# Linear attention in a decoder layer: the causal mask from DVE to ACT and GpSimd, and half of each feature map from DVE to GpSimd

## The reference, cut to what matters

```python
def _feature_map(t, K):
    f = jnp.einsum('hdf,bhld->bhlf', K, t)
    feats = jnp.concatenate([jax.nn.softmax(f, axis=-1), jax.nn.softmax(-f, axis=-1)], axis=-1)
    return jnp.maximum(feats, EPS)
q = _heads(x @ Wq); k = _heads(x @ Wk); v = _heads(x @ Wv)
qf = _feature_map(q, Kq)
kf = _feature_map(k, Kk)
kv = jnp.cumsum(kf[:, :, :, None, :] * v[..., None], axis=2)
o = jnp.einsum('bhlf,bhldf->bhld', qf, kv)
z = jnp.einsum('bhlf,bhlf->bhl', qf, jnp.cumsum(kf, axis=2)) + EPS
o = o / z[..., None]
```

## Time and profile before

| | |
|---|---|
| median of 3 runs | 1231.16 us (1226.87 to 1235.7) |
| time of the profiled execution | 1229.25 us |
| its span in the trace | 1227.0 us |
| linear attention, first part of the span | to about 540 us |
| busy over the span: PE, DVE, ACT, POOL | 91%, 78%, 50%, 31% |
| mean granted clock of PE | 0.982 of full speed |

### The profile page before, as it was taken

The page is one execution under the profiler, slowest core; times in us unless marked ns, Lnnn a source line. Parts: engine busy times, 40 slices in busy tenths (PEclk is TensorE's granted clock), DMA queues, the critical chain, the costliest instruction groups (busy, mean ns, idle before and its releaser), DMA issues. The chain is left out here.

```text
span 1227.0 us, 30062 instructions
## 1 busy us (share of the span) xinstructions
PE 1117.3 (91%) x11860; PEld 719.6 (59%) x11861; DVE 962.1 (78%) x1769; ACT 611.1 (50%) x1166; POOL 377.3 (31%) x355
## 2 busy tenths in 40 slices
PE   6698898899899999879999999999999957999996
PEld 5577777777788878643443344334444334666765
DVE  6889978987888788888788677877889556777757
ACT  4233343334333433227777677776788822444443
POOL 4432245222522222113201320222110414656651
PEclk9899999999999999999999999999999988999998
DMA  7100001000400000524720570065050144221225
GB/s 240 41 8 1 2 28 53 2 1 1 80 2 2 1 1 2 81 59 81 152 34 8 114 146 2 9 127 108 2 211 3 53 80 145 65 64 60 63 62 205
DMA packets 60045, 73.65 MB, mean 60 GB/s; under 512 B 14404, under 2 KB 51140, under 8 KB 59188
## 3 DMA queue, kind: packets, MB, share of 16 engines
q1 hardware_dynamic: 56132, 61.56, 21.0%
q0 software_dynamic: 3792, 10.36, 2.7%
HBM read 52.86 MB, written 18.78 MB: 58 GB/s over the span
## 5 line engine op out<-in xcount | busy, mean ns | idle before, releaser
L1791 DVE TENSOR_REDUCE neg_max<-pS 128x1 f32<-128x1024 f32 x238 | 284.9, 1220 | 56.2 <-PE pS L1574 56.0
L1706 ACT ACTIVATE pt<-pR 128x512 f32<-128x512 f32 x512 | 286.5, 600 | 80.1 <-PE pR L1597 75.3
L1597 PE MATMUL pR<-qs,ks 100*32 100x512 bf16 x2048 | 191.2, 383 | 3.1 <-ACT pt L1706 1.6
L1574 PE MATMUL pS<-ks,qs 100*32 100x512 bf16 x1904 | 145.9, 381 | 5.1 <-issue 1.9
L1611 PE MATMUL b_pO<-pt,b_v 128*32 128x512 f32 x1024 | 135.9, 605 | 2.9 <-ACT pt L1706 2.3
L1597 PEld LDWEIGHTS pR<-qs,ks 100*32 100x32 bf16 x2048 | 56.2, 96 | 95.3 <-issue 25.6
L324 POOL TENSOR_TENSOR kf<-kf,fsum 128x2048 f32<-128x2048 f32 (+1 forms) x17 | 58.2, 3422 | 163.8 <-DVE fsum L933 163.8
L324 POOL TENSOR_TENSOR qs<-qs,fsum 128x2048 f32<-128x2048 f32 (+1 forms) x17 | 58.5, 3446 | 142.7 <-DVE fsum L933 142.7
L1453 POOL COPY qs<-max_rows 3x512 bf16<-3x512 bf16 x60 | 36.6, 610 | 209.3 <-ACT max_rows L1699 206.3
L745 ACT COPY qfT<-pT 128x512 f32<-128x512 f32 x64 | 37.3, 582 | 122.7 <-PE pT L466 122.7
L1574 PEld LDWEIGHTS pS<-ks,qs 100*32 100x32 bf16 x1904 | 51.4, 97 | 74.3 <-issue 35.7
(11 more groups left out here) (376 smaller groups left out, 2270.8 us busy)
## 6 DMA issues: line engine op xcount, KB each, us to landing
qs<-q_scr SPq DMA_DIRECT2D x24, 256.0 KB
ks<-k_scr SPq DMA_DIRECT2D x7, 768.0 KB
k_scr<-f SPq DMA_DIRECT2D x18, 256.0 KB, 2.8
ks<-in_L_ffn_w_dram SPq DMA_DIRECT2D x2, 2048.0 KB, 11.1
ks<-in_L_ffn_w_dram SPq DMA_DIRECT2D x4, 1024.0 KB, 8.5
ks<-y_rows SPq DMA_DIRECT2D x16, 256.0 KB, 5.1
ks<-k_scr SPq DMA_DIRECT2D x6, 512.0 KB
cx<-in_ctx_dram SPq DMA_DIRECT2D x3, 768.0 KB, 12.3
```

Source lines behind the costliest of these rows:

```text
L1574: ins = pe.matmul(pS1[q:q + XV, slot, 512 * half:512 * half + 512], qs[0:KR, bass.ds(par, 1), h, P * t + q:P * t + q + XV].rearrange("r a ...
L1597: ins = pe.matmul(ring[bank][q:q + XV, :], ks[0:KR, bass.ds(par, 1), h, P * j + q:P * j + q + XV].rearrange("r a n -> r (a n)"), qs[0:KR, ...
L1706: nc.scalar.activation(pt[:, j % 2, i, :], ring[bank], ACT.Exp).then_inc(exp_done, 1)
L1791: nc.vector.tensor_reduce(neg_max[:, hg % 2, u // G, u % G:u % G + 1], pS1[:, u % 2, :], AX_X, ALU.max, negate=True).then_inc(max_done, 1)
```

## The change

The mask is split in two. ACT copies the scores from PSUM into am (`scores_copy`, signal `a_copied`), and POOL multiplies am in place with the causal triangle (`mask`, signal `a_masked`). PE may write the next scores into pA after `a_copied`; `outputs` still waits for `a_masked`. Of the feature maps (from turn 2 on for k, from turn 1 on for q) DVE writes only f - max, together with the small difference min - max of each head (`low_less_high`); POOL's `other_side` subtracts the one from the other, which gives min - f, and signals `shifted`, on which the exponential waits. The bank is free for PE after DVE's part alone (`drained`). POOL's constants move from ahead of the first turn into it. ACT's `v_copy` of half 0 moves ahead of `scores_copy(t, 3)`.

```diff
+                def other_side(m, t, half_of, par):
+                    pool.wait_ge(drained[m], 2 * (t - POOL_FROM[m]) + half_of + 1)
+                    hs = slice(8 * half_of, 8 * half_of + 8)
+                    nc.gpsimd.tensor_tensor(feat[m][:, par, hs, HD:F2],
+                                            low_less_high[:, m, hs].unsqueeze(2).broadcast_to([P, H // 2, HD]),
+                                            feat[m][:, par, hs, 0:HD], ALU.subtract).then_inc(shifted[m], 1)
...
+                def mask(t, g):
+                    wait(pool, a_copied, 4 * t + g + 1)
+                    pool.wait_ge(s_k, 8)
+                    nc.gpsimd.tensor_tensor(am[:, g % 2], am[:, g % 2], causal[:, :].unsqueeze(1).broadcast_to([P, G, P]),
+                                            ALU.mult).then_inc(a_masked, 1)
+
+                mask(0, 0)
                 scale(0, 1, 1)
...
-                        if not (last and c == TB - 1):
-                            scale(1, TB * b + c + 1, (c + 1) % 2)
+                        t, par = TB * b + c, c % 2
+                        has1, has2 = not (last and c == TB - 1), not (last and c >= TB - 2)
+                        mask(t, 1)
+                        if has1:
+                            other_side(1, t + 1, 0, 1 - par)
+                            other_side(1, t + 1, 1, 1 - par)
+                        if (b, c) == (0, 0):
+                            constants()
+                        mask(t, 2)
+                        if has1:
+                            scale(1, t + 1, 1 - par)
+                        mask(t, 3)
                         if (b, c) == (0, TB - 1):
                             split_k(0)
                             split_k(1)
-                        if not (last and c >= TB - 2):
-                            scale(0, TB * b + c + 2, c % 2)
+                        if has2:
+                            other_side(0, t + 2, 0, par)
+                            other_side(0, t + 2, 1, par)
+                        if has1:
+                            mask(t + 1, 0)
+                        if has2:
+                            scale(0, t + 2, par)
                         if (b, c) == (0, TB - 1):
                             split_k(2)
                             split_k(3)
...
                 def project_q(t, half, par):
-                    wait(pe, shifted[0], 2 * t + half + 1)
+                    bank_drained(pe, 0, t, half)
...
                 def chunk_scores(t, g):
...
-                    wait(pe, a_masked, 4 * t + g)
+                    wait(pe, a_copied, 4 * t + g)
...
+                def scores_copy(t, g):
+                    wait(act, a_done, 4 * t + g + 1)
+                    wait(act, o_done, 4 * t + g - 1)
+                    nc.scalar.copy(am[:, g % 2], pA[:, :, :]).then_inc(a_copied, 1)
...
                         f_copies(t, 1)
+                        scores_copy(t, 1)
...
                         f_copies(t, 2)
                         if has1:
                             exponentials(1, t + 1, 0, 1 - par)
+                        scores_copy(t, 2)
...
-                    nc.vector.tensor_tensor(feat[m][:, par, hs, 0:HD], f,
-                                            hi[:, m, hs].unsqueeze(2).broadcast_to([P, H // 2, HD]), ALU.subtract)
+                    if t >= POOL_FROM[m]:
+                        nc.vector.tensor_tensor(low_less_high[:, m, hs], lo[:, m, hs], hi[:, m, hs], ALU.subtract)
+                    ins = nc.vector.tensor_tensor(feat[m][:, par, hs, 0:HD], f,
+                                                  hi[:, m, hs].unsqueeze(2).broadcast_to([P, H // 2, HD]),
+                                                  ALU.subtract)
+                    if t >= POOL_FROM[m]:
+                        ins.then_inc(drained[m], 1)
+                        return
...
-                            if g < G - 1:
-                                mask(t, g + 1)
...
-                        if has1:
-                            mask(t + 1, 0)
```

More of the change, by code:

```diff
@@ L100, in linear_attention @@
         lo = sb("lo", [P, 2, H])
+        low_less_high = sb("low_less_high", [P, 2, H])
         fsum = sb("fsum", [P, 2, 2 * H])
@@ L163, in linear_attention @@
         shifted = [sem("k_shifted"), sem("q_shifted")]
+        drained = [sem("k_drained"), sem("q_drained")]
         expd = [sem("k_exp"), sem("q_exp")]
@@ L169, in linear_attention @@
         fT_ready = [sem("kT"), sem("qT")]
-        a_done, a_masked = sem("a_done"), sem("a_masked")
+        a_done, a_copied, a_masked = sem("a_done"), sem("a_copied"), sem("a_masked")
         d_done, s_upd = sem("d_done"), sem("state")
@@ L214, in linear_attention, with bank_drained @@
         HALVES = (slice(0, H // 2), slice(H // 2, H))
+        POOL_FROM = (2, 1)
+        def bank_drained(eng, m, t, half_of):
+            if t < POOL_FROM[m]:
+                eng.wait_ge(shifted[m], 2 * t + half_of + 1)
+            else:
+                eng.wait_ge(drained[m], 2 * (t - POOL_FROM[m]) + half_of + 1)
         with nc.Block() as block:
@@ L330, in _ @@
                         scale(m, 0, 0, hs, half_of)
-                scale(0, 1, 1)
[L333 to L347, removed]
+                def mask(t, g):
[3 more added lines that the diff above has]
+                                            ALU.mult).then_inc(a_masked, 1)
@@ new lines, in _, with constants @@
+                mask(0, 0)
+                scale(0, 1, 1)
+                def constants():
+                    pool.memset(last_row[:, :], 0.0).then_inc(s_k, 1)
+                    pool.wait_ge(s_k, 9)
+                    pool.affine_select(out=last_row[:, :], in_=last_row[:, :], compare_op=ALU.not_equal, fill=1.0,
+                                       base=-(KR - 1), pattern=[[0, 1]], channel_multiplier=1).then_inc(s_k, 1)
+                    pool.memset(q_aug[:, :], 0.0).then_inc(s_k, 1)
+                    pool.memset(zero[:, :], 0.0).then_inc(s_k, 1)
+                    pool.memset(max_parts[:, :, :, :], 0.0).then_inc(s_k, 1)
+                    pool.wait_ge(s_k, 12)
+                    pool.wait_ge(s_c, 48)
+                    for s in range(2):
+                        nc.gpsimd.tensor_copy(ck[:, s, :].rearrange("p (d h) -> p d h", h=XH),
+                                              ck_raw[:, s, :].rearrange("p (h d) -> p d h", h=XH)).then_inc(c_turned, 1)
+                    for k in range(KD):
+                        nc.gpsimd.tensor_copy(cq[:, k, :].rearrange("p (d h) -> p d h", h=XH),
+                                              cq_raw[:, k, :].rearrange("p (h d) -> p d h", h=XH)).then_inc(c_turned, 1)
@@ L448, in project_q @@
                 def project_q(t, half, par):
-                    wait(pe, shifted[0], 2 * t + half + 1)
+                    bank_drained(pe, 0, t, half)
                     project(1, half, par, proj[1])
                 def project_v(t, half, par):
-                    wait(pe, shifted[1], 2 * t + half + 1)
+                    bank_drained(pe, 1, t, half)
                     project(2, half, par, v_proj)
@@ L589, in turn_maxima @@
                     pe.wait_ge(prep_copied, PREPARED + 1)
-                    pe.wait_ge(a_masked, 4 * T)
+                    pe.wait_ge(a_copied, 4 * T)
                     turned = pA[:, :, :].rearrange("p h n -> p (h n)")
@@ L799, in _ @@
                 f_copies(0, 0)
+                scores_copy(0, 0)
                 exponentials(0, 1, 1, 1)
@@ L817, in batch @@
                             exponentials(1, t + 1, 1, 1 - par)
+                            v_copy(t + 1, 0, 1 - par)
+                        scores_copy(t, 3)
                         prepare(prep, 4)
-                        if has1:
-                            v_copy(t + 1, 0, 1 - par)
                         prepare(prep, 5)
@@ L846, in batch @@
                             exponentials(0, t + 2, 1, par)
+                        if has1:
+                            scores_copy(t + 1, 0)
                 batch(0, False)
@@ L938, in clamp @@
                                             ALU.max).then_inc(f_ready[m], 1)
[L940 to L945, removed]
                 def update(b, c, g):
@@ L1070, in _ @@
                 shift(0, 1, 1, 1, own)
-                dve.wait_ge(s_k, 6)
-                mask(0, 0)
                 denominators(0, 1, 1, own)
```

## The result

The changed kernel takes 1310.4 us (median of four runs, 1309.62 to 1310.8) against 1231.01 us (1226.87 to 1235.7): ratio 1.0643, 95% interval 1.0604 to 1.0682. Forecast were 1291 us and a range of 1257 to 1316. The profiled execution took 1310.69 us with a span of 1308.5.

What follows compares the result with a forecast made beforehand. The prediction took PE to lead, losing time to DVE, and the change to delay each turn's last outputs through POOL's order. Terms of +51, -9, +14.5, +5, +2 and -2 gave +61.5 on 1229.25: 1291 us, range 1257 to 1316.

Steps and rivals of the forecast that it cites:

- O3: The last outputs of a turn (group 3) on PE, forecast 21.6 us into the turn against 18.2 before, +3.4.
- Behind O3: PE's part of a turn after O3: 11.1 us, claimed to stay because PE waits there only for x_rest (0.92).
- a rival at 0.13: PE's granted clock falls behind the new waits, 3.4 us each in 7 turns: +24, 1315 us; chance 0.13.
- the sum: Terms added over the attention turns: +51, -9, +14.5, +5, +2, -2, together +61.5 on 1229.25, making 1291 us.
- turns 4 and 8, splits: POOL's two splits ahead of the group 1 mask delay PE: +14.5 us for both turns, bounds 10 and 18.
- turns 5, 9, 13, power: The variance's power heads POOL's order, waits for DVE's x1_normalise and delays the group 1 mask: +1.7 each, +5 us.
- turn 0, beyond O3's delay: POOL's constants now stand ahead of turn 0's group 2 mask: +2 us.
- The chain to O3: Steps from k scaling through shift, other_side, exponential, sum, q scaling and group 3 mask, putting O3 at 21.6 us.
- The meetings at the port: DVE and POOL block each other: the small difference behind k scaling, other_side behind the clamp; without both, O3 about 19.4, +1.2.
- The rival that had no meetings: The small difference slips past POOL and other_side past the clamp: +30, 1259 us; chance 0.20.
- The relief of DVE: Rival: a shorter DVE removes PE's waits if q scaling starts by 12.0 us into the turn: 1209 us; chance 0.05.
- the two waits: PE's waits on DVE for the mask ahead of the next scores (8.8) and the state (7.5), some 16 us.

Runs made afterwards that it cites:

- PE kept busy: The changed kernel with extra transposes of the identity, which nobody reads, ahead of the outputs where PE waits for a mask: 1292.69 us.
- when spread: The changed kernel with the 24 steps of POOL's six splits set one to three at a time between the maps' instructions: 1296.09 us.
- the run with POOL's whole order: The changed kernel with only POOL's order changed: group 3 mask before q scaling, splits spread, power, constants and turn 0's group 1 mask moved: 1223.1 us.
- the sides alone: The changed kernel with masks back on DVE straight from PSUM, without ACT's copies; POOL still makes the maps' negative side: 1245.97 us.
- the masks alone: The changed kernel with both sides of the feature maps back on DVE; ACT still copies scores and POOL masks them: 1293.7 us.
- with the mask of group 3 first: The changed kernel with one line of POOL's order moved: the group 3 mask ahead of the next q map's scaling: 1250.84 us.
- the two fastest runs: POOL's whole order changed plus the minimum over the positive side replacing the difference: 1215.86 us; the same with DVE's x1_normalise step moved to turn 6: 1216.35 us.
- the better order: POOL's whole order changed, with the minimum and x1_normalise moved: 1216.35 us; beside it the same with masks back on DVE, without ACT's copies: 1237.05 us.

## Why the prediction came out as it did

The direction and the mechanism were right: POOL's order, not its load or DVE's, sets O3. Where the forecast fell short by 19 us is the step "Behind O3 PE waits only for `x_rest` (0.92), so these 11.1 us stay." They did not stay, because of the clock, which I had as a rival at 0.13 and left out of the sum. With PE kept busy the changed kernel takes 1292.7 us, where the sum without the clock said 1291; with that rival's +24 it said 1315, and 1310.4 came. That 1292.7 lies so near to 1291 is in part luck: the clock was still at 0.97 there, and O3's delay, which the sum had too long, and turn 0, which it had too short, offset each other. The price of 3.4 us a wait and seven turns was near to what the fills showed: 2.7 us in turn 10, and 2 to 3.3 us in seven turns. There is luck in this too, since the stretch of the earlier trace rows that gave the price holds a second wait, of 2.60 us at 51.15. I should have made it part of the forecast: the sum itself put a wait of 3.7 us into each turn, and the earlier trace rows showed what one wait of 5.2 did.

| step | forecast, us | shown, us |
|---|---|---|
| O3 after the turn's first transposes | 21.6 | 21.1 (21.1 with PE kept busy) |
| behind O3 | 11.1 | 13.8 (11.1 with PE kept busy) |
| turns 4 and 8, splits | +14.5 | 14.3 come back when spread, clock included |
| turns 5, 9, 13, power | +5 | about +3.5 |
| turn 0, beyond O3's delay | +2 | +4.6 (7.4 in all) |
| turn 11 | 0 | 0 (32.74 and 32.77) |
| turn 15 | -2 | -1.9 |
| clock | 0 | 17.7 or more |

*The chain to O3.* Its first steps came to 0.1 us: the scaling of k at 2.13 to 5.75 (forecast 2.2 to 5.8), the difference waiting until 5.8 (5.9). Then `shift` of half 1 started at 8.1 instead of 8.5, and the second `other_side` ended at 12.2 instead of 12.9; the mask took 1.26 where I had 1.16. So O3 comes +2.8 a turn instead of +3.4. With PE kept busy turns 6, 10 and 12 took 2.8 us longer than before from residual to residual, just this delay. Turns 1, 2, 3, 7, 11 and 14 took 0.0 to 2.6 longer, so that some 8 us were covered there; the sum had 9 covered. The rows of the table do not add up to the 79.4 us, since the clock stands in several of them.

*The meetings at the port.* They are there, as rows above show, and removing the first one gave 6.9 us. My bound without both, +1.2 a turn, took the first at 1.1 us and left out that `normalise` still meets POOL, which the sum itself had in it; O3 of turn 10 gained 0.7. The rival that had no meetings is refuted by the rows. Only the first of them was removed; what the clamp's meeting costs was not tried.

*Turn 0.* Its residual started at 91.58 instead of 84.23. I counted the constants by the mask of group 2 alone. In the trace that wait is 4.6 us long, and 3.6 of the 7.4 us came back in the run with POOL's whole order (residual at 87.98):

```profile
73.86 0.93 PE L543 MATMUL pO<-v,am 128*64 128x66 f32 x12 [4.64 <-POOL am L352]
```

The masks on POOL make most of it: with the sides alone the residual stood at 86.97, at a clock of 1.00 from 62 us on, and with the masks alone at 93.25, at 0.84 (the changed kernel: 0.88). How it divides between their waits and the clock was not tried.

*Turns 4 and 8.* PE stood 9.57 and 9.03 us at `outputs` of group 1 where I said 8. The sum counts 9.8 us for two splits, though 10.3 less 0.9 is 9.4. Turn 4's wait:

```profile
217.84 1.15 PE L543 MATMUL pO<-v,am 128*64 128x66 f32 x16 [9.57 <-POOL am L352]
```

*The power.* Turns 9 and 13 took 37.5 us from residual to residual where turns 10 and 12 took 34.8. Before, they were 0.5 and 1.0 us longer than these already, so that the power makes 2.2 and 1.6 of it; turn 5, 2.2 longer than turn 6 before and 1.9 after, shows none. Ahead of the masks, but with the mask of group 3 first, turns 9 and 13 took 31.6 and 31.5, with the power behind the mask of group 2 both took 28.6; turns 10 and 12 took some 28 in both runs.

*The relief of DVE.* The rival gave 1209 if O3 had its mask by 16.8 us into the turn, and put against it "every row of the chain". For the changed kernel that held. With the order mended (and the minimum in place of the difference) O3 of turn 10 stands at 16.78 and the time is 1216:

```profile
355.89:372.67 16.78, 16.78 (x237) 14.91 (x237) 14.60 (x26) 8.74 (x15) 13.09 (x8) 1.00 0.01 2
372.67:383.71 11.04, 10.11 (x91) 8.91 (x87) 7.25 (x13) 4.32 (x7) 4.30 (x3) 1.00 0.00 0
```

PE is busy through the whole first part. So the price of 20 us was near: the two fastest runs lie 16 and 21 us below the kernel before beside them, the run with the order alone 14. Its condition had a second way in, which I did not name: not an earlier scaling, but the mask ahead of it. The 16 us that I counted for the two waits left one line of PE's waits before out, the state's first update in a batch:

```profile
PE pDW L484 <- DVE state L952: 4.9, 6, 1.1
```

With it they are 21 us, and the masks on POOL gave 20.7 in the better order.

*The rest.* Of the signs that I had named, a turn of 32 to 33 us without special work failed: it took 34.8, and 32.1 with PE kept busy. PE's longest wait a turn (3.94, for POOL), the start of the q scaling (16.1 us into turn 10) and the mean of the difference held (0.65 us, here from 100 to 530 us):

```profile
L972 DVE TENSOR_TENSOR low_less_high<-lo,hi 128x8 f32<-128x8 f32 x47 | 30.3, 646 | 1.6
```

DVE's busy time over the span fell by 27.5 us (962.1 to 934.6) and not by 60. What it stands blocked makes most of that: these 47 instructions alone took 30.3 us, where 0.17 each would be 8. From the last residual to the end the kernel took 684 us after 688 before, and 684 to 690 in the experiments, so cross attention and experts kept their length.

## What to carry to other kernels

Where work moves to another engine, its place in that engine's order can count for more than its length: here the place of one line was worth 60 us, on an engine that was half idle. Put the short step for which PE waits ahead of the long one that has slack, and cut long blocks into steps. And where a forecast puts a wait into PE's path, it must also price the slow clock behind it: with waits of 3 to 4 us a turn here, that was a fifth of the whole loss or more.

## What the runs showed of the hardware

- Filling PE's waits with useless transposes made the kernel 17.7 us faster. Waits of 3.2 and 3.9 us, in stretches at 0.99 and 1.00, were followed by 0.76 and 0.75 over the 13.6 and 13.8 us behind them; with the wait of 3.9 us filled but for 1.2, the stretch behind it stood at 1.00. That a wait as short as this would be followed by the lower clock I had not expected, having only seen one of 5.20.
- POOL's mask, with two full operands, took 1.29 us in the mean (82.6 us for 64), its subtraction with one of them broadcast along the row 1.04 in the median of the 28 for the k map (1.039 to 1.047):

```profile
L352 POOL TENSOR_TENSOR am<-am,a_causal 128x512 f32<-128x512 f32 x64 | 82.6, 1291 | 70.9 <-ACT am L793 70.9
```
